# Megabyte copies of the time step moved from SyncE's to ScalarE's DMA queue, with deeper staging around them, in a two-layer kernel with a selective scan

## The reference

```
x = x + attention(layernorm(x)) + ffn(layernorm(x))          # layer 0
h  = rmsnorm(layernorm(x)); u, z = split(h @ in_proj_w)       # layer 1, mixer
u  = silu(causal_conv(u)); dt_r, B, C = split(u @ x_proj_w)
dt = softplus(dt_r @ dt_proj_w + dt_proj_b); A = -exp(A_log)
for t:  state = exp(dt_t * A) * state + dt_t * u_t * B_t      # 256 channels x 16 states
        y_t   = sum over states of state * C_t
y  = (y + u * D) * silu(z);  mixer = y @ out_proj_w
experts = (silu(x@Ws1) * (x@Ws3) @ Ws2 + top-2 of 8 routed experts) / 3
x  = x + mixer + experts
```

## Time and profile before

| | |
|---|---|
| median of 3 runs | 1425.01 us (1411.26 to 1438.17) |
| profiled execution | 1406.75 us, of which the span from first to last instruction is 1404.8 us |
| TensorE busy, granted clock | 904.7 us (64%), 0.77 of full speed |
| VectorE busy | 944.3 us (67%) |
| ScalarE busy | 506.9 us (36%) |
| GpSimd busy | 717.7 us (51%) |
| DMA moved | 192.23 MB, 137 GB/s mean |

### The profile page before, as it was taken

How to read it: one execution, slowest core, us unless ns; L and a number is a source line. 1 busy time by engine, 2 the same in 40 slices (tenths; PEclk the granted TensorE clock), 3 DMA queues, 4 the chain that set the end, 5 groups by cost and what they waited for, 6 DMA issues and landing times. The chain is left out here.

```text
span 1404.8 us, 12618 instructions
## 1 busy us (share of the span) xinstructions
PE 904.7 (64%) x3460; PEld 415.0 (30%) x3460; DVE 944.3 (67%) x1288; ACT 506.9 (36%) x842; POOL 717.7 (51%) x547
## 2 busy tenths in 40 slices
PE   4587887786875544365774775766684774764543
PEld 1122332232322211133433433433443443421111
DVE  2577677677674511566776677769786687679874
ACT  1121221221221112364464454455464464454321
POOL 1110120210445046356556556549797588559997
PEclk8687878976877766687987897988897897875555
DMA  5974574662613042656666666657676676655662
GB/s 143 218 169 124 120 185 134 154 163 57 153 39 98 23 138 66 134 129 164 146 147 152 141 160 163 152 155 160 152 171 152 151 173 149 154 156 105 128 139 56
DMA packets 102833, 192.23 MB, mean 137 GB/s; under 512 B 13259, under 2 KB 68108, under 8 KB 90348
## 3 DMA queue, kind: packets, MB, share of 16 engines
q1 hardware_dynamic: 91500, 183.00, 52.8%
q0 software_dynamic: 11264, 8.43, 3.5%
HBM read 146.74 MB, written 32.06 MB: 127 GB/s over the span
## 5 line engine op out<-in xcount | busy, mean ns | idle before, releaser
L1452 POOL TENSOR_TENSOR hc<-hs,c_rep 128x512 f32<-128x512 f32 x256 | 369.3, 1523 | 219.4 <-DVE hs L1710 219.1
L1703 DVE TENSOR_TENSOR p_du<-p_du,b_rep 128x512 f32<-128x512 f32 x256 | 175.6, 686 | 170.4 <-PE p_du L1821 170.2
L1710 DVE TENSOR_TENSOR_SCAN hs<-slots,p_du 128x512 f32<-128x512 f32 x168 | 205.1, 1221 | 18.3 <-ACT slots L1578 2.7
L1821 PE MATMUL p_du<-block_in,spread 96*128 96x512 bf16 x256 | 118.4, 467 | 148.9 <-DVE hs L1710 85.3
L1578 ACT ACTIVATE slots<-slots,a_neg 128x512 f32<-128x512 f32 x168 | 116.9, 720 | 92.2 <-DMA slots<-dt_rows 92.1
L447 POOL TENSOR_TENSOR sc<-ex,ex_part 128x1024 f32<-128x1024 f32 x8 | 17.0, 2129 | 213.2 <-ACT ex_part L535 213.2
L1488 POOL DMA_INDIRECT y_xr<-moe_sums,position x64 | 106.2, 1660 | 35.1 <-issue 32.8
L1710 DVE TENSOR_TENSOR_SCAN hs<-decays,p_du 128x512 f32<-128x512 f32 x88 | 107.4, 1221 | 21.3 <-POOL hc L1452 13.8
L679 DVE TENSOR_TENSOR value_prod<-p_eb,v 128x512 f32<-128x512 f32 x128 | 83.8, 684 | 46.0 <-PE p_eb L959 45.5
L1837 PE MATMUL p_g<-ident,xg 128*128 128x128 f32 x96 | 26.0, 363 | 129.9 <-DMA xg<-moe_rows 127.1
L1821 PEld LDWEIGHTS p_du<-block_in,spread 96*128 96x128 bf16 x256 | 26.5, 105 | 266.6 <-DVE hs L1710 152.2
(11 more groups left out here) (186 smaller groups left out, 1742.9 us busy)
## 6 DMA issues: line engine op xcount, KB each, us to landing
slots<-dt_rows SPq DMA_DIRECT2D x42, 1024.0 KB
qb<-rq_rows SPq DMA_DIRECT2D x32, 1024.0 KB, 13.2
decays<-dt_rows SPq DMA_DIRECT2D x22, 1024.0 KB
wm<-in_wmoe SPq DMA_DIRECT2D x48, 384.0 KB, 14.7
moe_rows<-zeros SPq DMA_DIRECT2D x8, 774.0 KB, 6.1
xg<-moe_rows SPq DMA_DIRECT2D x48, 129.0 KB, 15.1
stack<-ex_part SPq DMA_DIRECT2D x96, 64.0 KB
block_in<-y_part SPq DMA_DIRECT2D x192, 32.0 KB
```

The lines of the kernel that those rows point to most:

```text
L1452: nc.gpsimd.tensor_tensor(hc[:, k % NA], hs[:, k % 4], c_rep[:, p], ALU.mult).then_inc(hc_done.sem, 1)
L1703: nc.vector.tensor_tensor(p_du[:, k % 2], p_du[:, k % 2], b_rep[:, p], ALU.mult).then_inc(dbu_done.sem, 1)
L1710: nc.vector.tensor_tensor_scan(hs[:, k % 4], decays[(8 * (b - 1) + k // 4) % NQ][:, bass.ts(j, T)], p_du[:, k % 2], 0.0, ALU.mult, ALU.add ...
L1821: nc.tensor.matmul(p_du[:, k % 2], spread[:, i], block_in[:, s, j], start=True, stop=True).then_inc(du_full.sem, 1)
```

## The change

Four edits that go together:

1. **Megabyte copies.** `load_decays` moves from SyncE's program to ScalarE's, so its DMAs are started by ScalarE and queue there. There are NQ = 4 buffers instead of 3. Inside a batch a copy is started at k = 1, 5, 9, 13, 17 (for the quarters 3 to 7), and at k = 21, 25, 29 the first three of the next batch.
2. **Projections a batch ahead.** z now has a staging tile `zr`, as u has `ur`. `project_z` for batch b + 2 runs at k = 27, 29 instead of for b + 1 at k = 5, 7. The rest of the preparation moves up: SiLU from k = 9 to 5, `x_proj` from 12 to 8, `dt_proj` from 14, 16 to 10, 12, softplus from 18, 19, 21 to 14, 15, 17, `steps` from 22, 24 to 17, 19, the parts from 24 to 27 to 19 to 22, the two `store_dt` from 23, 25 to 18, 20, and the `stack` of the next batch from 25, 27, 28 to 21, 22, 23.
3. **Six row buffers.** `xg` has NX = 6 buffers. The load of the rows waits for the tile six before, no longer for the tile four before; the wait for that one stands between the load of the rows and that of the weights.
4. **B and C in two steps.** `store_bc` at k = 10 starts the store; `repeat_bc` at k = 16 starts the loads.

The core of the diff:

```diff
-        NQ = 3
+        NX = 6
+        NQ = 4
...
             def load_tile(j, v):
                 grp, i = divmod(j, NTILE)
                 r = j % NR
-                if j >= NR:
-                    sp.wait_ge(down_done.sem, down_done.at(tile_unit[j - NR]))
-                    sp.wait_ge(os_done.sem, os_done.at(j - NR + 1))
+                if j >= NX:
+                    sp.wait_ge(os_done.sem, os_done.at(j - NX + 1))
...
-                sp.dma_start(xg[:, r], moe["rows"][grp][256 * i:256 * i + 256].rearrange("(s p) c -> p s c", p=128)).then_inc(xg_in[r].sem, 16)
+                sp.dma_start(xg[:, j % NX], moe["rows"][grp][256 * i:256 * i + 256].rearrange("(s p) c -> p s c", p=128)).then_inc(xg_in[j % NX].sem, 16)
+                if j >= NR:
+                    sp.wait_ge(down_done.sem, down_done.at(tile_unit[j - NR]))
+                    hold(sp)
...
-                    if new and k % 4 == 0 and k < 24:
-                        load_decays(b, k // 4 + 2)
...
+                        if k == 10:
+                            store_bc(b + 1)
+                        if k == 16:
                             repeat_bc(b + 1, 1 - p)
-                        if k == 23:
-                            store_dt(b + 1, 0)
-                        if k in (25, 27, 28):
-                            stack(b + 1, 0, (25, 27, 28).index(k))
-                        if k == 25:
-                            load_decays(b + 1, 0)
-                            store_dt(b + 1, 1)
-                        if k == 29:
-                            load_decays(b + 1, 1)
+                        if k in (18, 20):
+                            store_dt(b + 1, (k - 18) // 2)
+                        if k in (21, 22, 23):
+                            stack(b + 1, 0, k - 21)
...
+            def load_decays(b, q):
+                n = 8 * (b - 1) + q
+                s, i = divmod(q, 4)
+                if n >= NQ:
+                    c, last = divmod(n - NQ, 8)
+                    act.wait_ge(scanned.sem, scanned.at(c + 1, 4 * last + 4))
+                elif n >= 2:
+                    for kk in range(2):
+                        act.wait_ge(sent[kk], 16 * GT)
+                act.wait_ge(dt_out[s].sem, dt_out[s].at(b))
+                hold(act)
+                rows = dt_d[b % 2, s, 8 * i:8 * i + 8].unsqueeze(1).to_broadcast([8, N, 4 * T])
+                act.dma_start(decays[n % NQ], rows).then_inc(decays_in[n % NQ].sem, 16)
...
+                    if new and k % 4 == 1 and k < 20:
+                        load_decays(b, (k + 11) // 4)
+                    if nxt and k % 4 == 1 and k > 20:
+                        load_decays(b + 1, (k - 21) // 4)
...
+                    if k == 5:
+                        silu_u_z(b + 1, q)
```

More of the change, by code:

```diff
@@ L1153, in layer1 @@
         by_row = slots[:].rearrange("p r c -> p (r c)")
-        decays = [sb("decays", [128, 4 * T])[:], by_row[:, 0:4 * T], by_row[:, 4 * T:8 * T]]
+        decays = [sb("decays0", [128, 4 * T])[:], sb("decays1", [128, 4 * T])[:], by_row[:, 0:4 * T], by_row[:, 4 * T:8 * T]]
         wm = sb("wm", [128, NR, 3 * FF1])
-        xg = sb("xg", [128, NR, 2, D + 1])
+        xg = sb("xg", [128, NX, 2, D + 1])
         xgt = sb("xgt", [128, 2, 256])
@@ L1217, in layer1 @@
         wm_in = [count(f"wm_in{i}", 1, 16) for i in range(NR)]
-        xg_in = [count(f"xg_in{i}", 1, 16) for i in range(NR)]
+        xg_in = [count(f"xg_in{i}", 1, 16) for i in range(NX)]
         xg_turned = count("xg_turned", 1)
@@ L1272, in _ @@
         def _(sp):
-            start(sp, [*xt_in, *ht_in, bc_out, bc_in, *stacked, *dt_out, *decays_in, *wm_in, *xg_in, *os_out])
+            start(sp, [*xt_in, *ht_in, bc_out, bc_in, *stacked, *dt_out, *wm_in, *xg_in, *os_out])
             sp.wait_ge(ready1, 2)
@@ L1331, in wait_decays, with store_bc @@
                 hold(sp)
[L1333 to L1349, removed]
+            def store_bc(b):
                 sp.wait_ge(prep_free.sem, prep_free.at(b, XD))
@@ L1381, in prologue @@
                 sp.dma_start(xr[:], moe["xr"].rearrange("b p t d -> p b (t d)")).then_inc(xr_in, 16)
+                store_bc(1)
                 repeat_bc(1, 0)
-                store_dt(1, 0)
-                load_decays(1, 0)
+                for s in range(ST):
+                    store_dt(1, s)
                 for i in range(3):
                     stack(1, 0, i)
-                store_dt(1, 1)
-                load_decays(1, 1)
             def batch(b, p, old, new, nxt):
@@ L1511, in batch @@
                         gate_y(b, p, 0)
-                    if nxt and k in (22, 24):
-                        steps(b + 1, q, (k - 22) // 2)
+                    if nxt and k in (17, 19):
+                        steps(b + 1, q, (k - 17) // 2)
                     if (b, k) in bring:
@@ L1522, in _ @@
         def _(act):
-            start(act, [prep_free, z_done, u_done, sp_exp, sp_ln, part1, part2, da_done, g_read, xg_copied, os_done])
+            start(act, [prep_free, z_done, u_done, sp_exp, sp_ln, part1, part2, da_done, g_read, xg_copied, os_done, *decays_in])
             act.wait_ge(w_loaded, 16 * n_loads)
@@ L1596, in weigh @@
                 for i in range(2):
-                    ins = nc.scalar.activation(os[:, j % 2, i], p_o[:, bass.ts(i, 128)], ACT.Copy, scale=xg[:, j % NR, i, D:D + 1])
+                    ins = nc.scalar.activation(os[:, j % 2, i], p_o[:, bass.ts(i, 128)], ACT.Copy, scale=xg[:, j % NX, i, D:D + 1])
                 ins.then_inc(os_done.sem, 1)
             def prologue():
-                convolved(1, 0)
-                convolved(1, 1)
-                copy_out(1, Z0, sz[:, 0, 0])
-                copy_out(1, Z1, sz[:, 0, 1])
+                for s in range(ST):
+                    convolved(1, s)
+                for s in range(ST):
+                    gated(1, s)
                 silu_u_z(1, 0)
@@ L1611, in prologue @@
                 first_part(1, 0)
+                for q in range(3):
+                    load_decays(1, q)
                 second_part(1, 0)
-                convolved(2, 0)
-                convolved(2, 1)
+                for s in range(ST):
+                    convolved(2, s)
+                for s in range(ST):
+                    gated(2, s)
                 decay(1, 0)
@@ L1897, in prologue @@
                     project_u(2, n, range(CONV))
+                for n in range(ST):
+                    project_z(2, n)
                 spread_du(1, 0)
```

67 lines of the change are left out of this document (35 added, 32 removed).

## The result

The changed kernel takes 1432.53 us (median of 20 runs, 1420.74 to 1443.14), the kernel before 1426.01 us in the runs taken beside it (20 runs, 1409.0 to 1439.57). The ratio is 1.0077, with a 95% interval of 1.0047 to 1.0108: slower by a little (under 1%), where 1320 us was forecast, and outside the range of 1270 to 1384. The profiled execution took 1432.75 us with a span of 1430.8, against 1406.75 and 1404.8 before; that one was among the fastest of its runs, so the spans differ by more (26 us) than the medians do (6.5).

What follows compares the result with a forecast made beforehand. VectorE, nearest to full, idled 30 us of each batch, mostly waiting for TensorE, which waited for rows. Terms -41 - 73.5 - 3 + 12 + 5 - 2 = -102.5 gave 1304, scaled and stated as 1320 us; range 1270 to 1384.

Steps and rivals of the forecast that it cites:

- The megabyte copies themselves: Eight copies a batch, 10 us each beside other traffic, 80 per batch against 89 to 92 available: hidden, by little.
- waits for TensorE: Inside batches 1 to 6, VectorE's 103.5 us of waits fall to 5 per batch as rows start earlier: 73.5 us saved.
- Boundaries: At batch ends, moving the next batch's `stack` up removes VectorE's wait before its first step: 41 us saved, at least 30.
- Waits for GpSimd: At GpSimd's first fetch, which waits for the last tile's store: the store may land sooner, 3 us saved, 0 to 14.
- VectorE, +12: VectorE's operations take longer beside a GpSimd that pauses less in shorter batches 4 to 6: 12 us added, 0 to 24.
- ScalarE, +5: ScalarE's 8 DMA starts per batch fit; waits in its stream and SiLU's lump are charged 5 us, 0 to 15.
- rival C: ScalarE becomes the pace: its in-order waits make decays late and give back 96 us, time 1400, scaled 1418; chance 0.05.
- Start-up, 0 (-3 to +4): Before the first step: the second part moves to about 560, the last `stack` copies hardly move; 0, from -3 to +4.
- Sum: All terms together: -102.5 us, 1304 on the profiled execution's scale, 1321 scaled to the runs' median, given as 1320 us.
- B: Small copies get slower beside megabyte copies, rows land at 28 us: 1451, scaled 1470, slower than before; chance 0.04.
- A: The shared DMA engines limit tile batches at 167 GB/s to 101 us: 1363, scaled 1380; chance 0.14.
- The rule weighed: Skill's rule: copies from different starters share 16 DMA engines, saving only starting time; another, turns between queues, supported the forecast.

Runs made afterwards that it cites:

- a1_copies_on_sync: The changed kernel with the megabyte copies started by SyncE again, four buffers and all other edits kept; 1342.70 us.
- the fastest kernel: The changed kernel with SyncE starting the megabyte copies and each row of the steps stored twice (16 source rows, 8 repeats); 1277.32 us.
- a3_small_rows: The changed kernel with each megabyte copy as four copies with rows of 2 KB, on ScalarE's queue; 1296.97 us.
- b5_rows_twice: The changed kernel with dt's rows stored twice, so a megabyte copy has 16 source rows read 8 times, on ScalarE's queue; 1287.76 us.
- a2_only_queue: The kernel before with only the megabyte copies moved to ScalarE's queue, three buffers, the same steps; 1472.48 us.

## Why the prediction was wrong

**The failed step is "The megabyte copies themselves": "So they are hidden, by little."** It priced a copy by its own length, 8.6 us alone, 10 with company. That length was right (10.5 by the packets), and hidden they are: before, decays waited 141.3 us in 40 times for a copy, now 18.9 in 4, and no scan waits for a decay. But the time did not fall by it. What a copy costs is what it does to the small copies beside it, and for that the sum had no term; with copies on sixteen engines the same change takes 1288 us. The row was on the page: a share of 0.51 with one copy alone. I read it as "so room is left". Half the engines were full, half were empty. The second step that failed stands in the 73.5 us of waits for TensorE: SyncE "no longer queues megabyte copies ahead of rows" was counted as a gain. Taking them off SyncE's queue cost 90 us. The obstacle was the engines behind both queues.

*Boundaries, -41.* Right in place. (Step k = 0 is a batch's first.) The first `p_du` of batches 2 to 7 comes without a wait, in the changed kernel as in a1_copies_on_sync; at batch 8 the changed kernel waits 11.88 us, a1 0.81. But the time did not go: in the changed kernel, batches 2 and 5 among others, VectorE waits for TensorE, and that for rows, at k = 11 or 12 and at 30 instead.

*Waits for TensorE, -73.5, 5 us a batch left.* In the changed kernel 136.7 us are left (140.9 before), 23 a batch. With the queue given back 69.7 are left, 12 a batch, and with the copies spread too 30.3, 5 a batch. So 5 a batch exists, but for another edit than the one I counted on.

*Waits for GpSimd, -3.* 2.6 us in batches 1 to 6, 7.0 before; but the longest wait of all batches, 16.92 us, came in batch 7, where I kept "places of both unchanged" and did not ask what a slow start ahead of the store does.

*VectorE, +12.* 465.8 us busy in batches 1 to 6, 464.1 before, and 462.4 in the fastest kernel with batches of 87 us. The charge was wrong; dearer operations did not grow with density. The reading behind it was wrong too: batch 4, where VectorE was busy 84.1 us, had the less busy GpSimd (75.9 us, against 82.6 in batch 5). A single operation makes 3.1 us of the difference (line 1678 took 5.72 us in batch 4 and 2.58 in batch 5).

*ScalarE, +5, and rival C.* Right that it does not set the pace inside the batches: its starts took 0.59 us, and no scan waits for a decay. With 32 starts a batch in place of 8, in a3_small_rows, the scans wait 2.7 us for it in the whole span.

*Start-up, 0 (-3 to +4).* It cost 7.9 us. The second part ran at 562.25, not at 560, behind ScalarE's wait for dt and its three starts, and three copies at once run beside twelve `stack` copies, whose starts took 11.18 us, 7.57 before. Spreading the copies does not cure it (first scan at 580.57 in b5_rows_twice).

*Sum.* Without the move to ScalarE's queue the sum comes near, 1342.7 against 1320 and inside the range, but partly by luck: 12 us a batch stayed where 5 were counted, and the 12 us for VectorE were not needed. The rest of the change is worth 5.6% as long as the copies stay narrow; that it is cover for late rows and steps is argued.

**Rivals.** B had the mechanism, slower pieces beside a copy, and got 0.04. Its price rested on a threshold for the median (landing over 25.7 us); the median rose only to 17.1, while single ones rose to 34.0, and TensorE waits for single ones. It also counted rows alone, not `block_in` nor SyncE's starts. A fell: 198 GB/s at a share of 0.83 were sustained over six batches, where it had 167 as the limit. **The rule weighed**: of the two rules of the Trainium skill, the one on shared engines was the nearer: a second starter gained nothing. It does not give a loss, and the loss was 90 us. Turns between queues I took to favour the rows. The runs show both: rows land in 10.3 us with two queues in a2_only_queue (15.1 before) and in 17.1 in the changed kernel. One piece of the other queue carries sixteen times the bytes of a row's (8192 against 516), which may be why turns don't help; no run shows it.

## What to carry to other kernels

A DMA share of one half with one transfer alone is a question, not a comfort: multiply pieces by their time, divide by the length, and see how many engines worked. Look at the outermost dimension of source and destination; a broadcast of few rows runs on few engines and here it delayed small copies on whatever queue it was started. Widen or shorten such copies first, and only then move them between queues or schedule around them: here that one edit gave 9% to the kernel before (1288.3 us), and left 0.9% for all the scheduling (1277.3).

## What the runs showed of the hardware

Pieces of 8 KB took 548 ns in the mean on eight engines, 561 on sixteen and 366 on four, all on ScalarE's queue (on SyncE's, on eight, 485 in a1_copies_on_sync and 545 before); pieces of 2 KB 102 on eight, so 8 KB in four pieces took 408 ns, a quarter less than in one. A DMA start on SyncE, 0.4 us in the median, took up to 9.9 us while another queue kept eight engines full, up to 6.9 us with the copies on its own queue (a1_copies_on_sync), and at most 0.57 us for the rows' line with 2 KB pieces on ScalarE's queue (a3_small_rows). TensorE's granted clock, a mean over its two levels (1.2 and 2.4 GHz), was 0.88 of full speed in the six batches of the fastest kernel, where TensorE was busy 413.8 of 522.5 us, and 0.82 in those of the changed one, with 436.2 of 644.6.
